# Local transformer: the loops over tiles of the attention written out, and the first tile projected by itself

## The reference, cut to what matters

```python
h = shift_token(x)                       # second half of the features from the token before
q, k, v = split(h @ wqkv)                # 8 heads of 64
q, k = rotary_xpos(l2norm(q) * qs, l2norm(k) * ksc)
o = local_attention(q, k, v)             # windows of 64, each looks at itself and the one before
x = x + o @ wo
h = layernorm(shift_token(x)) @ w1 + b1
a, g = split(h)
x = x + (a * gelu(g)) @ w2 + b2
```

## Time and profile before

| | |
|---|---|
| median of 3 runs | 3523.84 us (3522.46 to 3531.91; all: 3531.91, 3523.84, 3522.46) |
| the profiled execution's own time | 3529.88 us |
| its span, first to last instruction | 3528.1 us |
| mean granted clock of PE | 0.916 |
| PE busy | 2837.1 us (80%), 22065 instructions |
| DVE busy | 2477.9 us (70%) |
| ACT busy | 1755.7 us (50%) |
| POOL busy | 1837.4 us (52%) |
| DMA queues for instructions | q8: 157 packets, 2.57 MB; q14: 93 packets, 0.76 MB |

### The profile page before, as it was taken

The page is one execution under the profiler, slowest core; times in us unless marked ns, Lnnn a source line. Parts: engine busy times, 40 slices in busy tenths (PEclk is TensorE's granted clock), DMA queues, the critical chain, the costliest instruction groups (busy, mean ns, idle before and its releaser), DMA issues. The chain is left out here.

```text
span 3528.1 us, 64431 instructions
## 1 busy us (share of the span) xinstructions
PE 2837.1 (80%) x22065; PEld 1677.4 (48%) x22143; DVE 2477.9 (70%) x4050; ACT 1755.7 (50%) x3567; POOL 1837.4 (52%) x1184
## 2 busy tenths in 40 slices
PE   3678468558999995899899994677677499999998
PEld 1111256443444442677567752223222277757774
DVE  5599646548777773677577755798699677667764
ACT  3544124134555563577467732543444277637662
POOL 3499211030111101888188822697299498729871
PEclk8699769679999997999999996899799799999999
DMA  3355000032222210112111210343144111212121
GB/s 90 82 157 148 8 7 8 0 103 73 43 40 41 41 26 23 34 42 46 29 36 41 43 25 5 115 158 110 48 166 157 37 41 41 44 24 43 40 44 39
DMA packets 176118, 202.74 MB, mean 57 GB/s; under 512 B 108358, under 2 KB 122396, under 8 KB 175388
## 3 DMA queue, kind: packets, MB, share of 16 engines
q1 hardware_dynamic: 175868, 199.41, 21.8%
HBM read 138.36 MB, written 9.44 MB: 42 GB/s over the span
## 5 line engine op out<-in xcount | busy, mean ns | idle before, releaser
L319 POOL TENSOR_TENSOR arena<-arena 128x1024 f32<-128x1024 f32 x192 | 451.4, 2352 | 61.7 <-DVE arena L336 34.3
L1446 DVE TENSOR_REDUCE causal_peak_parts<-psum 128x1 f32<-128x512 f32 (+3 forms) x608 | 375.8, 659 | 105.3 <-PE psum L1303 60.1
L2051 POOL TENSOR_TENSOR arena<-arena,w_minus_half 128x16 f32<-128x16 f32 x128 | 372.5, 2911 | 130.8 <-DVE arena L1958 130.8
L1412 ACT ACTIVATE arena<-psum 128x512 f32<-128x512 f32 (+1 forms) x608 | 303.8, 595 | 229.9 <-PE psum L1325 108.3
L1893 ACT ACTIVATE arena<-psum,arena 128x128 f32<-128x128 f32 x1024 | 277.9, 380 | 258.2 <-DVE arena L1967 258.2
L336 DVE TENSOR_TENSOR_SCAN arena<-psum,arena 128x1024 f32<-128x1024 f32 x160 | 366.0, 2289 | 28.4 <-POOL arena L319 28.4
L289 ACT ACTIVATE psum<-arena,w_A 128x1024 f32<-128x1024 f32 x192 | 214.4, 1118 | 248.9 <-DVE arena L336 211.9
L2058 POOL TENSOR_TENSOR arena<-arena 128x1024 f32<-128x1024 f32 x124 | 292.1, 2356 | 6.7 <-DVE arena L1952 6.7
L1738 PE MATMUL psum<-w_layer_wqkv,arena 128*128 128x512 f32 x512 | 259.2, 629 | 6.6 <-DVE arena L1952 5.2
L262 PE MATMUL psum<-arena,m_sel 96*128 96x512 bf16 x384 | 117.6, 388 | 181.6 <-DVE arena L351 154.8
L1963 DVE COPY arena<-psum 128x512 f32<-128x512 f32 x128 | 88.5, 691 | 240.2 <-PE psum L1750 240.2
(11 more groups left out here) (331 smaller groups left out, 6652.3 us busy)
## 6 DMA issues: line engine op xcount, KB each, us to landing
arena<-scan_rows_large SPq DMA_DIRECT2D x128, 512.0 KB, 3.7
arena<-arena SPq DMA_DIRECT2D x256, 130.0 KB, 2.5
arena<-scan_rows_small SPq DMA_DIRECT2D x128, 256.0 KB, 3.8
arena<-causal_parts SPq DMA_DIRECT2D x288, 64.0 KB
causal_parts<-arena SPq DMA_DIRECT2D x8, 768.0 KB, 5.3
arena<-Z SPq DMA_DIRECT2D x128, 32.0 KB, 1.8
arena<-Z SPq DMA_DIRECT2D x32, 128.0 KB
arena<-in_c_pads SPq DMA_DIRECT2D x4, 896.0 KB
```

Source lines behind the costliest of these rows:

```text
L319: pool.tensor_tensor(inputs[:, s % 2], b_lane[:, s % U], du(*runs[o]), ALU.mult).then_inc(input_up.sem, 1)
L1412: act.activation(PT[:, kt % 2, heads[0]:heads[0] + len(heads), lo:hi], place, ACT.Exp, scale=SCALE).then_inc(probs.sem, 1)
L1446: dve.tensor_reduce(part[:, heads[0]:heads[0] + len(heads), qt, half:half + 1].rearrange("p h a -> p (h a)"), place[:, 0:len(heads) * size ...
L2051: pool.tensor_tensor(RN[:, s4, :], SS[:, s4, :], k.minus_half[:, 0:2 * HEADS], ALU.pow).then_inc(rn_in.sem, 1)
```

## The change

Both loops go: `in_steps` and `in_batches` call `step` for all 32 tiles with plain numbers, so every engine's program holds 32 written-out tiles in each of the four passes, and waits and addresses are constants. At the start of a stage (depth 0) PE turns tile 0 alone, projects its q, k and v, and only then turns tiles 1 to 3; ACT copies tile 0 alone (128 columns), squares and takes the values, and then copies tiles 1 to 3 (384 columns). Since tile 0's projection already writes bank 0, these transposes go to bank 7. Depth 1 keeps its form: four tiles, bank 0, one copy.

```diff
--- before.py
+++ after.py
@@ -1508,9 +1508,10 @@
         @block.tensor
         def _(pe):
             a = attention[0].tensor(pe)
-            a.turn_first()
+            a.turn_first(range(0, 1))
             a.project_first()
             a.values_first()
+            a.turn_first(range(1, 4))
             a.project_second()
             for depth in range(2):
                 u = units[depth].tensor(pe)
@@ -1524,9 +1525,10 @@
         @block.scalar
         def _(act):
             a = attention[0].scalar(act)
-            a.copy_first()
+            a.copy_first(0, 1)
             a.square_first()
             a.take_first()
+            a.copy_first(1, 4)
             for depth in range(2):
                 u = units[depth].scalar(act)
                 after = attention[1].scalar(act) if depth == 0 else None
@@ -1650,29 +1652,19 @@
     def outputs():
         return two(5).rearrange("p (b c) -> p b c", b=2)[:, :, 0:PAIRS * (HD + 1)].rearrange("p b (h d) -> p b h d", d=HD + 1)
 
+    first_bank = 0 if units else 7
+
     def in_steps(eng, step, after={}):
 
-        loops = (TILES - RING - AHEAD) // RING
-        for i in range(RING):
-            step(i, i, AHEAD, i)
-        with eng.Fori(1, 1 + loops) as p:
-            for s in range(RING):
-                step(p * RING + s, s, AHEAD, RING)
-        for i in range(RING + RING * loops, TILES):
-            step(i, i % RING, TILES - 1 - i, RING)
+        for i in range(TILES):
+            step(i, i % RING, min(AHEAD, TILES - 1 - i), min(i, RING))
             if i in after:
                 after[i]()
 
     def in_batches(eng, step):
 
-        loops = (TILES - RING - AHEAD) // TPB
-        for i in range(RING):
-            step(i, i, i, AHEAD, i)
-        with eng.Fori(0, loops) as p:
-            for s in range(RING, RING + TPB):
-                step(p * TPB + s, s % RING, s % TPB, AHEAD, RING)
-        for i in range(RING + TPB * loops, TILES):
-            step(i, i % RING, i % TPB, TILES - 1 - i, RING)
+        for i in range(TILES):
+            step(i, i % RING, i % TPB, min(AHEAD, TILES - 1 - i), min(i, RING))
 
     def sync(sp):
         def credit():
@@ -1718,11 +1710,11 @@
         return part
 
     def tensor(pe):
-        def turn_first():
+        def turn_first(tiles):
             pe.wait_ge(cs_in.sem, cs_in.at(0))
-            for i in range(RING):
+            for i in tiles:
                 pe.wait_ge(z_in[i].sem, z_in[i].at(64))
-                pe.transpose(bank[0][:, i * P:(i + 1) * P], ZS[:, i, :], k.ident).then_inc(h_up.sem, 1)
+                pe.transpose(bank[first_bank][:, i * P:(i + 1) * P], ZS[:, i, :], k.ident).then_inc(h_up.sem, 1)
 
         def turn_in(i, s4, outputs):
             pe.wait_ge(z_in[s4].sem, z_in[s4].at((i - s4 + RING) * 64 // RING if isinstance(i, int) else (i - s4 + RING) * 16))
@@ -1731,7 +1723,7 @@
             pe.transpose(bank[7][:, P:2 * P], ZS[:, s4, :], k.ident).then_inc(h_up.sem, 1)
 
         def project_qk(i, s4):
-            pe.wait_ge(h_in.sem, h_in.at(max(i + 1, RING) if isinstance(i, int) else i + 1))
+            pe.wait_ge(h_in.sem, h_in.at(RING if isinstance(i, int) and (units or i) and i < RING else i + 1))
             if not (isinstance(i, int) and i == 1):
                 pe.wait_ge(cs_in.sem, cs_in.at(i - 1 if isinstance(i, int) and i == 2 else i))
             for m in range(2):
@@ -1855,10 +1847,10 @@
         return part
 
     def scalar(act):
-        def copy_first():
-            act.wait_ge(h_up.sem, h_up.at(RING))
+        def copy_first(lo, hi):
+            act.wait_ge(h_up.sem, h_up.at(hi))
             act.wait_ge(v_up.sem, v_up.at(0))
-            act.copy(HT.rearrange("p s t -> p (s t)"), bank[0]).then_inc(h_in.sem, RING)
+            act.copy(HT[:, lo:hi, :].rearrange("p s t -> p (s t)"), bank[first_bank][:, lo * P:hi * P]).then_inc(h_in.sem, hi - lo)
 
         def copy_h(i, s4):
             act.wait_ge(h_up.sem, h_up.at(i + 1))
@@ -2215,7 +2207,7 @@
                 if ahead:
                     turn(u + 1, 1 - s)
                 if after and ahead == 1:
-                    after.turn_first()
+                    after.turn_first(range(4))
                 if after and not ahead:
                     after.values_first()
                 product(u, s, 2)
@@ -2252,7 +2244,7 @@
                 if ahead:
                     affine(u + 1, 1 - s)
                 if after and ahead == 1:
-                    after.copy_first()
+                    after.copy_first(0, 4)
                 gate(u, s, 2)
             if after:
                 after.take_first()
```

## The result

The changed kernel takes 3495.34 us (median of 6 runs, 3489.56 to 3498.66), the kernel before, run beside it, 3525.74 us (6 runs, 3519.64 to 3531.91). The time lies 4.7 us under the forecast's range. Its profiled execution took 3489.56 us, span 3487.6 us.

A forecast was written before the change was run, and what follows sets the result against it. PE's own instructions were taken to bound the steady tiles. Two stage starts (7.3 and 7.5 us) and pass 4's stop (7.3) sum to 22.1, off the profiled 3529.88: 3507.8, about 3508 us, range 3500 to 3517.

The forecast's parts named there:

- first stage, tile 0's transpose to tile 1's q and k: Start of the first transformer stage: projecting tile 0 alone brings PE's transposes of tile 1 7.3 us earlier (6.5 to 9.1).
- second stage, the same: Start of the second transformer stage: PE's transposes of tile 1 come 7.5 us earlier by the same chain (6.5 to 9.2).
- stop in pass 4: PE's jump back before tile 12 of pass 4: the wait for a lost instruction block goes, 7.3 us; lower bound 0.
- loops written out, apart from the stop: Looped tiles of all passes: removing register work and branches gains nothing, and fetching the added code costs 0.
- the lower pair: Known times 3522.5 and 3523.8 us of the kernel before, taken as runs without PE's stop at the jump in pass 4.
- rival E: PE's stop at the jump was there in every timed run; the median falls by all of 22.1, to 3501.7; chance 0.09.
- The two ways to 3508: Whole kernel: profiled 3529.88 less 22.1 gives 3507.8; median 3523.84 less 14.8 for the starts alone gives 3509.0.
- Rival A: PE's stop stays or moves, to stage 7's scan loops or a written-out block; 3515.1 us, chance 0.13.
- Rival B: Tile 1's projection at both stage starts runs at full clock, gains 8.3 and 9.2; 3505.1 us, chance 0.12.
- C: The two stage starts give less, 2.7 and 3.2 us, as tile 1's lost clock goes through unbuffered; 3516.7 us, chance 0.11.
- D: Tiles 12 to 19 of every pass: instruction fetching falls behind; slower, 3546.8 us at 1.5 us per block, chance 0.04.
- F: Every jump of PE stopped before, so 4 x 7.3 us go with the starts' 14.8; 3485.9 us, chance 0.01.

The follow-up runs named there:

- the two later profiles: The kernel before, profiled twice more with nothing changed; executions of 3522.29 and 3525.04 us.

## Why the prediction was wrong

**The terms held, the base did not.** Three traces each of the kernel before and of the changed one give these means:

| term | forecast | measured |
|---|---|---|
| first stage, tile 0's transpose to tile 1's q and k | 7.3 | 6.2 (32.78 to 26.58) |
| second stage, the same | 7.5 | 8.6 (34.11 to 25.50) |
| stop in pass 4 | 7.3 | 7.9 (7.3, 8.2, 8.1) |
| loops written out, apart from the stop | 0 | not told from 0 |
| sum | 22.1 | 22.7 |

Each start's term was off by 1.1 us, one too high and one too low, so that their sum, 14.8, came out exactly: that is luck. The first was too high because PE's way to tile 1's transposes grew (9.45 to 11.92 us in the first profile), where the forecast had kept its length. The changed kernel's start itself varies from execution to execution, from 25.35 to 27.79 us in the first stage and from 24.44 to 26.68 in the second.

The step that failed is "I take it that the lower pair ran without the stop". Four times were sorted into two pairs, 7.7 us apart, and the gap was given the size of the stop. With 17 runs of the kernel before in one job the times lie between 3514.04 and 3533.32, with no gap wider than 5.0 us, and one of 3527.65 in the first job lies inside that one; the stop is in all three traces, of executions of 3522.29, 3525.04 and 3529.88 us. So the sum had to come off the median: 3523.84 - 22.1 = 3501.7, which the forecast had as rival E with a chance of 0.09. The two ways to 3508 agreed because both leaned on the same error. The profiled execution was a long one by 6 us, for both routed stages were at their long end (132.2 and 132.9 us; in each of the two later profiles one of them was 7 us shorter), and the lower pair was taken to be free of a stop that it had.

That step accounts for 6.3 of the 12.7 us between 3508 and the measured 3495.3. It does not account for the rest: 3501.7 lies inside the stated range, and the measured time lies 6.4 us under it. For these the forecast had no term.

**What is left.** About 28 us measured, with an interval of 21 to 35, and 22.7 in the named terms. Inside the two transformer stages the traces differ by 25.5 us (sums of both stages: 1498.5, 1499.8, 1499.4 before; 1470.9, 1476.0, 1474.3 after). Of the 2.8 us beyond the terms, 0.5 is the time from the layernorm to tile 0's transpose in the second stage, and the rest stands in the gated units, where the means sum to 2.4 less but single traces go both ways (the last units of the launch took 97.6 and 99.0 us before, 97.6 to 101.2 after). Stages 1 to 5 have the same code and were 9.3 us shorter in the three traces of the changed kernel, in stages 2 and 4 by the granted clock. Stage 7, whose code is also the same, was 1.6 us longer (638.8 to 639.1 us from its layernorm to the next before, 639.8, 640.0 and 641.8 after). Together the spans of the traces differ by 33.3 us. Whether what lies outside the terms is chance, or depends on something that the change touches, these runs do not settle, and the cause of these 5 to 6 us stays open; the ratio came out at 0.992 three times.

**Point by point.** Right: PE bounds the steady tiles, so register work is free; the stop at the jump hangs on where PE's code lies and goes with the jump (that a block has to be fetched again stays a reading); POOL gets a new wait of 2.7 us for tile 1; both gains reach the end. Missed: the transposes of tile 1 came 6.2 and 8.8 us earlier in the first pair of profiles, not 7 to 8, and the six runs lie within 9.1 us of each other, not 2. The SP issue of 1.74 us sat in the forecast's rows for the second stage unseen, inside the 9.5 us between the transposes of tiles 0 and 3 (8.3 in the two later profiles), and was taken as a fixed part. Rival A (the stop stays or moves) did not come: there is no gap in the changed kernel's passes, and stage 7 grew by 1.6 us, far less than a stop. Rival B's full clock did not come in the first stage, where tile 3's projection even fell to half. C and D are refuted: the starts gave 14.8 us, and the written-out tiles 12 to 19 take 8.26 us in every pass, with packets of q8 among them (six in pass 1 from 1497 to 1559). F is refuted by the passes without a stop.

## What to carry to other kernels

A hardware loop with a long body (here 1733 instructions of PE) can cost several microseconds at one jump and nothing at the next; look for one long "issue" at a loop's head with instruction packets around it, and try a few idle instructions ahead of the loop before writing everything out. (A shorter body was not tried.) Where the first tile of a pipeline waits for a copy that covers several, send it alone: the gain is what the next tile allows, and that tile is late next. Take a forecast off the median of the timed runs, and don't read a cause into the spread of four of them.

## What the hardware showed beyond that

- The size of a stop hangs on the place too: 3.2 to 6.1 us from 35 to 58, 7.3 to 8.3 us from 99 to 184. Part of it lies in the tile after the gap, which took up to 12.9 us, and part of it is the lower clock after PE's pause (2.6 of 8.2 us in one profile, 1.7 of 7.3 in another).
- SP's DMA issues are slower while an instruction packet of q8 is under way. In the first transformer stage of the kernel before, the shifted tile's third issue (L1691) took at most 0.92 us in 61 cases without such a packet and 1.47 us in the median of the 3 with one; the second (L1690) at most 0.62 us in 57 cases, and 1.16 in the median of 7, up to 1.8. Steady tiles keep their 8.26 us. At the start of the second stage in the first profile it put tile 0's projection 10.71 us after its transpose, against 9.54 in the two later ones, and the transposes of tile 1 came no later for it.
- Runs of one program spread by 19 us here (3514.04 to 3533.32). The granted clock in the routed blocks makes a good part of it: stages 2 and 4 each differ by 7 us from trace to trace.
